# Cross-attentions of a twelve-sublayer decoder: the maxima are turned ahead of both pairs of score products, and subtracted between them

## What is computed

```python
# L1X; L2X adds mask * -1e9 to the scores, L3X replaces masked scores by the smallest float
qh = (q @ Wq.T + bq).reshape(B, Lq, 16, 8)
kh = (kv @ Wk.T + bk).reshape(B, Lkv, 16, 8)
vh = (kv @ Wv.T + bv).reshape(B, Lkv, 16, 8)
scores = jnp.einsum('bqhd,bkhd->bhqk', qh, kh) * scale
attn = jax.nn.softmax(scores, axis=-1)
ctx = jnp.einsum('bhqk,bkhd->bqhd', attn, vh).reshape(B, Lq, 128)
out = ctx @ Wo.T + bo
```

## Time and profile before

| | |
|---|---|
| time, median of 3 runs | 5264.44 us (5246.1 to 5288.91) |
| the profiled execution | 5250.1 us, its span 5248.4 us |
| PE | 4404.1 us busy (84%) |
| DVE | 2698.8 us busy (51%) |
| ACT | 1905.3 us busy (36%) |
| POOL | 920.5 us busy (18%) |
| mean granted clock of PE | 0.891 of full |

### The profile page before, as it was taken

One profiled execution on the slowest core, in us unless ns is written; L12 is line 12 of the kernel. 1 busy time (PEld: TensorE's weight loads), 2 busy tenths in 40 slices (PEclk: granted clock), 3 DMA queues, 4 the chain that ended last, 5 costly groups with the idle time before them and its releaser, 6 DMA issues. The chain is left out here.

```text
span 5248.4 us, 63414 instructions
## 1 busy us (share of the span) xinstructions
PE 4404.1 (84%) x23432; PEld 2353.8 (45%) x23432; DVE 2698.8 (51%) x6209; ACT 1905.3 (36%) x3352; POOL 920.5 (18%) x804
## 2 busy tenths in 40 slices
PE   6898889888689888988868988898886898889887
PEld 3454444633435444463344544446334454444632
DVE  6555443643656544364365554436436555443743
ACT  3243222445324322344532432224453243222445
POOL 2121100222202110022221211002222021100222
PEclk8898899989789889987978988998897898899989
DMA  2000100000100010000010001000001000100000
GB/s 79 1 3 27 58 5 2 17 2 2 54 0 3 27 58 5 2 17 1 2 54 0 3 27 58 5 2 17 2 2 54 0 3 27 58 5 2 17 1 4
DMA packets 20900, 93.01 MB, mean 18 GB/s; under 512 B 5228, under 2 KB 14444, under 8 KB 17796
## 3 DMA queue, kind: packets, MB, share of 16 engines
q1 hardware_dynamic: 20580, 88.80, 4.5%
HBM read 86.70 MB, written 2.10 MB: 17 GB/s over the span
## 5 line engine op out<-in xcount | busy, mean ns | idle before, releaser
L217 POOL TENSOR_SCALAR rstd_e<-mean_var 128x4 f32<-128x4 f32 x120 | 27.3, 228 | 2497.2 <-DVE mean_var L183 2496.7
L2167 DVE TENSOR_TENSOR arena<-ps,arena 128x512 f32<-128x512 f32 x256 | 176.5, 691 | 464.4 <-ACT arena L2117 464.4
L2117 ACT ACTIVATE arena<-ps 128x512 f32<-128x512 f32 x288 | 172.0, 597 | 603.5 <-PE ps L2065 603.4
L1625 ACT ACTIVATE arena<-ps 77x512 f32<-77x512 f32 x384 | 196.4, 591 | 458.6 <-PE ps L1543 458.6
L2507 PE MATMUL ps<-w_even,w_odd 128*128 128x512 f32 x640 | 325.1, 655 | 26.9 <-issue 26.9
L2064 PE MATMUL ps<-xT,w_even 128*128 128x512 f32 x576 | 306.1, 613 | 3.1 <-DVE arena L2154 3.1
L2071 PE MATMUL ps<-arena,w_even 128*128 128x512 f32 x576 | 295.0, 594 | 7.0 <-DVE arena L2167 4.7
L766 PE MATMUL ps<-xT,w_even 128*128 128x512 f32 (+1 forms) x544 | 269.4, 618 | 0.4
L2065 PE MATMUL ps<-arena,w_even 128*128 128x512 f32 x512 | 264.4, 598 | 0.0
L206 DVE TENSOR_TENSOR y_tok<-ps,x_tok 128x512 f32<-128x512 f32 x72 | 49.4, 686 | 343.0 <-PE ps L704 265.4
L1803 PE MATMUL ps<-arena,w_odd 128*128 128x512 f32 x512 | 220.4, 592 | 0.0
(11 more groups left out here) (431 smaller groups left out, 9503.4 us busy)
## 6 DMA issues: line engine op xcount, KB each, us to landing
w_even<-in_w SPq DMA_DIRECT2D x4, 6916.0 KB, 19.0
w_even<-in_w SPq DMA_DIRECT2D x4, 3313.5 KB, 10.7
w_odd<-in_w SPq DMA_DIRECT2D x4, 2824.5 KB, 9.6
w_odd<-in_w SPq DMA_DIRECT2D x4, 2095.0 KB, 8.3
w_odd<-in_w SPq DMA_DIRECT2D x4, 2048.0 KB, 15.0
x_in<-in_x SPq DMA_DIRECT2D x10, 256.0 KB, 2.9
w_odd<-in_w SPq DMA_DIRECT2D x4, 577.0 KB, 4.1
result<-x_tok SPq DMA_DIRECT2D x8, 256.0 KB, 2.3
```

Source lines behind the costliest of these rows:

```text
L1625: nc.scalar.activation(m["PT"][j % 2][:, c, :], bank(2 + c)[0:KC, :], ACT.Exp, scale=scale)\
L2117: nc.scalar.activation(e_sg[i % 2], bank(i % 2), ACT.Silu).then_inc(e_silu.sem, 1)
L2167: j = nc.vector.tensor_tensor(e_h[i % 2], bank(2 + i % 2), e_sg[i % 2], ALU.mult)
```

## The change

Two things are moved, nothing is added and nothing is removed. In PE's queue `turn_max(i-1)` goes from behind `scores(i, 0)` to ahead of it, and `less_max(i-1)` from behind `scores(i, 1)` to ahead of it. In DVE's queue `by_head(i-1)` goes from between `maxima(i, 0)` and `maxima(i, 1)` to ahead of both.

```diff
@@ pe_context
                 for i in range(8 + 2):
+                    if 0 <= i - 1 < 8:
+                        turn_max(i - 1)
                     if i < 8:
                         scores(i, 0)
                     if 0 <= i - 1 < 8:
-                        turn_max(i - 1)
                         turned_scores(i - 1)
+                        less_max(i - 1)
                     if i == 1:
                         pe_turn_state(pe, PREV[L], 1)
                     if i < 8:
@@
-                    if 0 <= i - 1 < 8:
-                        less_max(i - 1)
                     if 0 <= i - 2 < 8:
                         heads(i - 2)
@@ dve_context
                 for i in range(8 + 2):
-                    if i < 8:
-                        maxima(i, 0)
                     if 0 <= i - 1 < 8:
                         by_head(i - 1)
                     if i < 8:
+                        maxima(i, 0)
                         maxima(i, 1)
                         split_max(i)
```

## The result

The changed kernel takes 5445.07 us (median of 4 runs, 5443.28 to 5452.9) against 5255.27 us for the kernel before on the same chip: a ratio of 1.036, with a 95% interval of 1.034 to 1.039. It is 190 us slower. Direction and mechanism were as forecast; one term of the sum, the clock, was much too small.

A forecast was written before the change was run, and what follows sets the result against it. It took a loop through PE and DVE, neither full, to bound the cross-attention rounds; 83 us of longer loop plus 46 of lowered clock made +129 on 5264, rounded to 5390 us, range 5325 to 5445.

The forecast's parts named there:

- the clock: Cross-attention rounds: longer PE pauses ahead of `turn_max` lower PE's granted clock in more rounds, +46 us.
- The ring: Cross-attention loop through PE and DVE, from `scaled` via `turn_max`, scores and maxima back to `scaled`; moved products lengthen it, +83 us.
- `by_head` is hidden: DVE's `by_head`, moved ahead of `maxima(i, 0)`, costs nothing behind PE's longer stretch; without that cover, 0.69 us.
- the CAST's collision with POOL: The split's first CAST stretches beside POOL's multiply; earlier `less_max` ends this, gaining 0.22 us a round in L1X, 0.42 in L3X.
- 29 more rounds of the 60 fall, 29 x 1.6: Sequences 3 to 7: 9 + 15 + 5 more rounds lose clock, each 1.6 us longer, +46 us.
- the second rival: In L2X's 2.5 us pause especially, the clock falls every round and stays down longer: 5442 us, chance 0.15.
- I leave both out: Round 1: half-clock products costing double, and the first `turn_max` no longer waiting for a pair of scores; neither counted.
- The rule of the Trainium skill: Pauses between PE's bursts of products are all short enough that no round loses its clock; the sum stays +83 us.
- the first rival: Cross-attentions: only the loop through PE and DVE grows, +83 us, and the clock holds: 5347 us, chance 0.2.

The follow-up runs named there:

- the filled version: The changed kernel with products that nothing reads (12, 22, 14 in L1X, L2X, L3X) ahead of `turn_max` in rounds 2 to 7: 5305 us, ratio 1.008.
- its own filled version: The kernel before with products that nothing reads (7, 14, 4 in L1X, L2X, L3X) between `scores(i, 0)` and `turn_max(i-1)`: 5213 us, ratio 0.993.

## Why the prediction was right or wrong

**What was right.** The ring and who is on it; that `turn_max` starts no sooner, that the moved scores leave PE's pause and lengthen it (1.54 us, forecast 1.5; in L3X 1.54 to 1.65, forecast 1.6; in L2X 2.6, forecast 2.5); that `by_head` is hidden (moved alone, without that cover, it costs 0.70 in L1X, forecast 0.69); that the CAST's collision with POOL goes; that the loss lies in the cross-attentions; and that the clock falls after the longer pauses. The direction was given 0.93, rightly.

**The ring: forecast 83, measured about 65 us.** Read at full clock in the filled version, 28 rounds of 0.61, 0.95 and 0.75 us make 65. The term that was too large is `less_max`, taken at 0.35. The moves made alone show it, at full clock. In L2X `turn_max` costs 0.74 and `less_max` 0.22 (forecast 0.72 and 0.35). In L3X they cost 1.00 and -0.28 (forecast 1.09 and 0.35 - 0.42 = -0.07). Their sums, 0.96 and 0.72, are the 0.95 and 0.75 of the whole change. L1X takes another path than forecast: the prediction had PE reach `scores(i, 1)` after DVE had released it (2.39 against 2.0), but PE's products overlap, and the release by `maxima(i, 0)` comes last. That makes 0.84 up to the second maxima instead of 1.07.

**The clock: forecast 46, measured about 125 us (190 - 65).** This is the step that failed: "29 more rounds of the 60 fall, 29 x 1.6". It has two factors. The count was somewhat low: 59 rounds fell against 23 before, 36 more. The price was the real error. The 1.6 us was read from rounds in which the clock was low for a part (0.77 and 0.82), and was carried over as if a fallen round always cost that. In the changed kernel the middle rounds lie above the full-clock length of the filled version by 1.7 us on average in L1X (7.96 against 6.24), 2.2 in L2X and 3.6 in L3X. That makes 150 us over the 60 rounds, against 38 that the kernel before lost by the same measure (against its own filled version): 112 more. The cause of the higher price is in the rows: the clock stays down for longer. In L1X a round at 0.50 costs 2.8 us against 1.1 at 0.74. In L3X the five middle rounds of a pass read 0.82, 0.55, 0.73, 0.58 and 0.50 and take 9.6 to 13.6 us; in a round like the one at 0.55 `heads` takes 3.65 us, `scaled` waits for it, and all of PE's products lie on the ring. This is the second rival in kind. It had 0.15, and its time of 5442 is 3 us from the median, but partly by luck: its sum was 83 + 95, where the runs give 65 + 125. Its mechanism was right, but its place was not: I looked for it in L2X, where the pause is longest, and it was worst in L3X, whose rounds leave PE the least idle time (busy 6.72 of 7.37 us at full clock) and had nearly all been at full clock before.

**The first two rounds: forecast 24 us of ring, measured 47.** They are 8 of each 28 rounds, so 8 x (0.85 + 1.07 + 1.02) = 24 of the 83 lie in them; what is special about round 1 was put at nothing ("I leave both out"). In round 1 the maxima of the first sequence are not split yet when PE gets there. Before, PE used that wait for `scores(1, 0)` and stood idle for 1.3 to 1.6 us in L1X, 0.8 in L2X and not at all in L3X. Now it is idle for 3.7, 3.2 and 2.2 us ahead of the first `turn_max`, and for 2.2 to 3.2 ahead of the second. The granted clock is lower than before in both rounds of L3X (0.50 against 0.76 to 0.84, then 0.78 against 1.00) and in the second of L2X (0.84 against 0.97 and more); in L1X it is lower in some passes only. The first two rounds of a run, summed over the passes, are 8, 13 and 26 us longer. If the ring costs there what it costs in the middle rounds, it is 19 of the 47, an estimate; the rest would be clock, and no run divides it.

The parts fit, all taken from the two profiles: middle rounds 47 of ring (20 x (0.62 + 0.98 + 0.74), by the means of the two filled versions) + 112 of clock, and 47 in the first two rounds are 206, the growth of the cross-attentions. The other sublayers give a few us back, which makes the 203 us between the two profiled executions; the medians are 190 apart.

**The rule of the Trainium skill** (TensorE: Matmul & The Clock Gate, the section on why this matters for your kernels), by which pauses this short leave the clock alone, had 0.2 as part of the first rival. The runs rule it out for this kernel: a pause lengthened by one DVE instruction cost some 100 us of clock, and filling pauses of 0.95 to 2.6 us brought the full clock back. Only the pauses ahead of the first `turn_max` of L1X and L2X, 3.7 and 3.2 us, are long by that rule, and all the 59 fallen middle rounds lie behind shorter ones.

## What to carry to other kernels

Before moving an instruction that waits ahead of one that doesn't, ask what fills the wait now: here the products that came out of the pause were paid twice, once on the ring and once in clock. Price a fallen clock by a round that is at half clock throughout, where every engine that waits for PE waits longer, and not by the mildest case in the trace; and look at the first round of a pipeline by itself. If PE has regular pauses of one or two us, a few products that nobody reads can be worth a try: here they gave 0.7 to 0.85%.

## What the runs showed of the hardware that I had not expected

- In the changed kernel 39 of 40 middle rounds of L1X and L3X, with pauses of 1.5 to 1.7 us, had a lowered clock, and all 20 of L2X, with 2.2 to 3.0 us. With 0.2 to 0.7 us, in the filled version of the kernel before, 0 of 40 rounds in L1X and L2X fell. The length of the pause is not the whole rule: in the version with the doubled reciprocal L1X had 1.98 us and kept the full clock in 9 of 20 rounds, and with `less_max` moved alone 11 of 20 rounds of L1X fell with 0.95 us or less, where 6 did before.
- The same pause goes with two lasting clocks: L3X with the order of before ran at full clock with a pause of 0.64 us, and at half clock, for five rounds in all four passes, with 0.61 to 0.62 us. There PE was busy 12.16 of 12.78 us, more of its time than at full clock (6.72 of 7.37).
- Where the clock falls in one sublayer moves with what came before it: sublayers that no edit touched changed by up to 13 us over the four passes (the self-attention of layer 3, ahead of L3X, was 13 us shorter in the changed kernel).
